# One gather tile in 64 moved from GpSimd to SyncE, row by row, in the last layer of a graph network

## The reference, cut to what matters

```python
s = s @ W_up_s * inv; v = einsum('nui,uw->nwi', v, W_up_v) * inv   # per node
h = silu(silu(edge_feats @ A1 + b1) @ A2 + b2)                     # per edge
w0, w1, w2, w3 = split(h @ A3, 4, axis=1)
ss, vs = s[sender], v[sender]                                      # the gather
mji = concat(ss*y_s*w0, (vs . y_v)/R3*w3, ss*y_v*w1, vs*y_s*w2)
message = segment_sum(mji, receiver) / 10
```

## Time and profile before

| what | value |
|---|---|
| runs | 7211.72 us median of 3 (7203.6 to 7215.84) |
| profiled execution, span from first to last instruction | 7212.5 us |
| gathers of the message layer, first start to last start | 6068.1 to 7146.5 us |
| the last block's first matmul | 7159.95 us |
| POOL busy in the whole span | 4972.2 us (69%) |
| DMA in the message layer | 22% of 16 DMA engines, 56 GB/s |

### The profile page before, as it was taken

One profiled execution on the slowest core, in us unless ns is written; L12 is line 12 of the kernel. 1 busy time (PEld: TensorE's weight loads), 2 busy tenths in 40 slices (PEclk: granted clock), 3 DMA queues, 4 the chain that ended last, 5 costly groups with the idle time before them and its releaser, 6 DMA issues. The chain is left out here.

```text
span 7212.5 us, 119527 instructions
## 1 busy us (share of the span) xinstructions
PE 5515.6 (76%) x30306; PEld 4153.5 (58%) x30345; DVE 4706.7 (65%) x20339; ACT 2265.8 (31%) x5973; POOL 4972.2 (69%) x5179
## 2 busy tenths in 40 slices
PE   5675667776777766777777776789899997889887
PEld 4442344555666555566656665666666665667665
DVE  7985668466666446666636666664544546888887
ACT  1044442211114311113421111543333333554454
POOL 5777765677777477777577777647576574777774
PEclk6687888788888878888878888889999998988898
DMA  9433352577777467767557777657566773222222
GB/s 306 135 79 88 78 114 52 155 204 207 206 208 218 149 186 210 208 203 216 175 165 210 208 208 206 204 164 211 166 208 188 210 208 93 56 57 56 56 57 54
DMA packets 911842, 1151.30 MB, mean 160 GB/s; under 512 B 143281, under 2 KB 676465, under 8 KB 911249
## 3 DMA queue, kind: packets, MB, share of 16 engines
q1 hardware_dynamic: 689440, 673.54, 30.9%
q0 software_dynamic: 202464, 461.07, 23.9%
q10 hardware_dynamic: 19346, 9.66, 0.5%
HBM read 882.09 MB, written 261.74 MB: 159 GB/s over the span
## 5 line engine op out<-in xcount | busy, mean ns | idle before, releaser
L500 POOL DMA_INDIRECT G<-table_kv,idx x2496 | 2383.7, 955 | 966.5 <-issue 753.8
L1710 DVE SCALAR_TENSOR_TENSOR sums<-ramp,place,bank 128x128 f32<-128x128 f32 x2496 | 717.4, 342 | 1192.0 <-PE bank L1629 1098.4
L1619 PE MATMUL bank<-ident,G 128*128 128x128 f32 x2496 | 637.9, 334 | 720.1 <-DMA G<-table_kv,idx 713.5
L2144 POOL DMA_INDIRECT G<-table_h,src_idx x864 | 828.4, 959 | 465.0 <-issue 252.0
L1598 ACT COPY slab<-bank 128x512 f32<-128x512 f32 x624 | 364.8, 585 | 2295.3 <-PE bank L1619 2294.6
L500 POOL DMA_INDIRECT G<-table_h,idx x832 | 826.3, 993 | 298.2 <-issue 226.7
L1629 PE MATMUL bank<-qT,slab 128*128 x4992 | 915.5, 341 | 100.3 <-issue 80.4
L1629 PEld LDWEIGHTS bank<-qT,slab 128*128 128x128 f32 x4992 | 803.1, 244 | 196.0 <-issue 195.2
L1619 PEld LDWEIGHTS bank<-ident,G 128*128 128x128 f32 x2496 | 377.6, 163 | 931.2 <-DMA G<-table_kv,idx 891.7
L1841 DVE TENSOR_SCALAR OH<-ramp,place,weight 128x128 f32<-128x128 f32 x2076 | 715.4, 354 | 15.6 <-issue 8.5
L2128 PE MATMUL bank<-sums,qT 128*128 128x418 bf16 (+1 forms) x3528 | 676.4, 334 | 38.7 <-DVE same L2051 13.9
(11 more groups left out here) (355 smaller groups left out, 9538.6 us busy)
## 6 DMA issues: line engine op xcount, KB each, us to landing
stash<-G SPq DMA_DIRECT2D x312, 512.0 KB
sums<-stash SPq DMA_DIRECT2D x624, 256.0 KB
sums<-adjacency SPq DMA_DIRECT2D x294, 522.5 KB
adjacency<-same SPq DMA_DIRECT2D x49, 1184.0 KB, 13.9
same<-adjacency SPq DMA_DIRECT2D x90, 522.5 KB
G<-table_kv,idx POOLq DMA_INDIRECT x2496
sums<-adjacency SPq DMA_DIRECT2D x48, 408.0 KB
table_kv<-G SPq DMA_DIRECT2D x72, 256.0 KB, 3.2
```

What stands on the lines that cost most here:

```text
L500: pool.indirect_dma_start(G[:, s, 0:width], None, tab, bass.IndirectOffsetOnAxis(ap=idx[:, s:s + 1], axis=0)).then_inc(c_gather[s].sem, 16)
L1619: ins = pe.transpose(bank[q % 2][:, (s % QUAD) * P:(s % QUAD + 1) * P], G[:, s, 0:D], ident[:])
L1710: ins = dve.scalar_tensor_tensor(scratch[:, s, :], ramp[:], place[:, n * QUAD + s:n * QUAD + s + 1], bank[2 + q % 2][:, s * P:(s + 1) * P] ...
L2144: pool.indirect_dma_start(G[:, s, 0:D], None, table[l], bass.IndirectOffsetOnAxis(ap=src_idx[:, DENSE + t:DENSE + t + 1], axis=0)).then_in ...
```

## The change

GpSimd no longer gathers slot 15 in the last turn of every four (`FAR_TURNS = 4`): 13 tiles of 832, the far tiles. SyncE fetches them. The host adds the source numbers laid out by tiles in rows (`src_rows`). For each far tile SP loads one such row into `far_src`, and in each of the four turns, at four places, loads eight source numbers into registers and issues eight DMAs, each of one row of 512 bytes from `table[0]` into one partition of `far_rows` (two buffers). At the end of the fourth turn it waits until all 128 rows have landed and copies `far_rows` into slot 15 of `G` with one DMA. DVE waits for that copy (`far_landed`) in place of the gather. POOL's loop is written out over four turns.

```diff
             @block.gpsimd
             def _(_e):
-                gather_loop(table[0], D)
+                with pool.Fori(0, FAR_TILES) as m:
+                    for u in range(FAR_TURNS):
+                        for q in range(QUADS):
+                            pool.wait_ge(c_idx.sem, c_idx.turn(m, FAR_TURNS * QUADS, u * QUADS + q + 1))
+                            pool.sem_inc(c_issue.sem, 1)
+                            for s in range(q * QUAD, (q + 1) * QUAD):
+                                if u < FAR_TURNS - 1 or s != FAR_SLOT:
+                                    pool.indirect_dma_start(G[:, s, 0:D], None, table[0],
+                                                            bass.IndirectOffsetOnAxis(ap=idx[:, s:s + 1], axis=0)).then_inc(c_gather[s].sem, 16)
...
+                def far_line(m):
+                    t = (m * FAR_TURNS + FAR_TURNS - 1) * SLOTS + FAR_SLOT
+                    sp.dma_start(far_src[0:1, m % 2, :], a["src_rows"][t:t + 1, :]).then_inc(far_src_in.sem, 16)
+
+                def far_part(i, part):
+
+                    m, k = i // FAR_TURNS, (i % FAR_TURNS * QUAD + part) * FAR_ROWS
+                    if k == 0:
+                        sp.wait_ge(far_src_in.sem, far_src_in.at(16 * (m + 1)))
+                        if m + 1 < FAR_TILES:
+                            far_line(m + 1)
+                        if m >= 2:
+                            sp.wait_ge(far_landed.sem, far_landed.at(16 * (m - 1)))
+                    _, nodes = nc.values_load_multi_w_load_instructions(
+                        far_src[0:1, m % 2, k:k + FAR_ROWS], engines=(SP,), min_val=0, max_val=NODES - 1,
+                        skip_runtime_bounds_check_because="sources are nodes")
+                    for r, node in enumerate(nodes):
+                        sp.dma_start(far_rows[k + r:k + r + 1, m % 2, :], table[0][bass.ds(node, 1), :]).then_inc(far_in[m % 2].sem, 16)
+
+                def far_tile(i):
+                    m = i // FAR_TURNS
+                    sp.wait_ge(far_in[m % 2].sem, far_in[m % 2].at(16 * P * (m // 2 + 1)))
+                    sp.wait_ge(c_msg.sem, c_msg.at(QUADS * i))
+                    sp.dma_start(G[:, FAR_SLOT, 0:D], far_rows[:, m % 2, :]).then_inc(far_landed.sem, 16)
+
+                far_line(0)
 
                 def turn(i, last):
                     for h in range(2):
                         sp.wait_ge(c_msg.sem, c_msg.turn(i, QUADS, 2 * h + 2 - QUADS))
                         sp.dma_start(ea[:, h, :, :].rearrange("p s c -> p (s c)"),
                                      a["edge_attrs"][:, bass.ds(i * SLOTS * 4 + h * HALF * 4, HALF * 4)]).then_inc(c_ea[h].sem, 16)
+                        far_part(i, 2 * h)
                         if not last:
                             sp.wait_ge(c_h1.sem, c_h1.turn(i, 2, h + 1))
                             features(h, (i * 2 + (h + 2)) * PAIR)
+                        far_part(i, 2 * h + 1)
+                    if i % FAR_TURNS == FAR_TURNS - 1:
+                        far_tile(i)
                 turns(turn)
...
                 def messages(i, turn_q):
                     j, h, q = turn_q % 2, turn_q % QUADS // 2, turn_q % QUADS
                     dve.wait_ge(c_rows.sem, c_rows.turn(i, QUADS, turn_q + 1 - QUADS))
+                    t = i + turn_q // QUADS
+                    far = (t + 1) // FAR_TURNS
                     for s in range(q * QUAD, (q + 1) * QUAD):
-                        dve.wait_ge(c_gather[s].sem, c_gather[s].turn(i, 16, 16 * (1 + turn_q // QUADS)))
+                        if s != FAR_SLOT:
+                            dve.wait_ge(c_gather[s].sem, c_gather[s].at(16 * (t + 1)))
+                        elif t % FAR_TURNS == FAR_TURNS - 1:
+                            dve.wait_ge(far_landed.sem, far_landed.at(16 * far))
+                        else:
+                            dve.wait_ge(c_gather[s].sem, c_gather[s].at(16 * (t + 1 - far)))
```

More of the change, by code:

```diff
@@ L98 @@
 KNOTS = BLOCKS + 1
+FAR_TURNS = 4
+FAR_TILES = TURNS // FAR_TURNS
+FAR_SLOT = SLOTS - 1
+FAR_ROWS = P // (FAR_TURNS * QUAD)
 assert CHUNK * CHUNKS == NP and CHUNK <= 512 and TILES % 8 == 0
@@ L104 @@
 assert 8 * ZERO_COLS >= ADJ_COLS and 8 * ZERO_COLS <= ADJ_PITCH and FIRST_BLOCKS * DENSE <= GROUP_COLS <= MASK_COLS and EXTRA_BLOCKS * HALF_DENSE <= MASK_COLS and TURNS_DENSE % 2 == 0 and P < SEEN
-assert sum(PIECE_LENGTHS) == TURNS and PT <= P and 3 * PIECES * P <= BLOCKS * ROW
+assert sum(PIECE_LENGTHS) == TURNS and FAR_TILES * FAR_TURNS == TURNS and FAR_ROWS * FAR_TURNS * QUAD == P and PT <= P and 3 * PIECES * P <= BLOCKS * ROW
 assert PART * X_PARTS == BLOCKS and NODES % BN == 0 and NODES // BN <= BLOCKS
@@ L203, in build_program @@
         per_slot = sb("per_slot", [P, 2, SLOTS])
+        far_rows = sb("far_rows", [P, 2, D])
+        far_src = sb("far_src", [P, 2, P], I32)
         stats = sb("stats", [P, BLOCKS, 6])
@@ L326, in build_program @@
         c_tp = signal("tp_psum")
+        far_src_in = signal("far_src_in")
+        far_landed = signal("far_tile_landed")
+        far_in = [signal(f"far_rows_in{k}") for k in range(2)]
         c_far = signal("distance")
@@ L2784 @@
         "src_tile": np.concatenate([tiles(src), np.zeros((P, SLOTS), src.dtype)], axis=1),
+        "src_rows": src.reshape(TILES, P),
         "dst_tile": tiles(dst),
```

## The result

| | kernel before | changed kernel |
|---|---|---|
| median, lowest, highest of 13 runs each | 7208.59 (7201.88 to 7215.84) us | 7190.18 (7180.83 to 7198.58) us |
| ratio, 95% interval | | 0.9975 (0.9968 to 0.9983) |
| profiled execution, span | 7212.5 us | 7179.0 us |

The change made the kernel 18 us faster, 0.25%, where 157 us slower was predicted. It went the way of the first rival: SP stayed hidden, and POOL's 13 gathers were the gain. The two profiled executions lie 33.5 us apart, but 20.1 us of that were gone before the message layer began: its first gather starts at 6048.0 us where it was 6068.1 us, and nothing ahead of it was changed.

A forecast was written before the change was run, and what follows sets the result against it. POOL's gathers bound the message layer, 83.0 us a group of four turns; SP's added work, 95.2 us against POOL's 81.7, would become the bound, adding 156.7 us to 7212.5 us: 7369 us, range 7195 to 7500 us.

The forecast's parts named there:

- the first rival: Message layer: SP stays hidden and POOL's gain of 16.9 us is real, giving 7196 us; chance 0.10.
- item 1 of what the change adds on SP: SP's 128 one-row DMAs a group: 0.19 us ahead plus 0.43 us issue, 0.62 us a row, 79.4 us.
- DMAs that back up: Rival on SP's queue: packs of eight rows issue at 0.60 us each, giving 7651 us; chance 0.14 from 0.50 us up.
- S: SP's in-order work for a group of four turns in the message layer, summed to 95.2 us.
- The eight numbers of a register load: SP's 16 loads of eight source numbers a group: 0.36 us each, 0.40 with gap, 6.4 us together.
- The register work ahead of a row: On SP before each row's DMA: gap, MOVE and ALU_OP for a new node number, 0.19 us.
- The landing at a group's end: SP stands still until the group's last row has landed: 2.0 us less the issue itself, 1.6 us.
- POOL's 1.297 us a gather: POOL's gather spacing in the message layer; 13 gathers fewer save 16.9 us if POOL remains the bound.
- the formula 13 x S - 1080.9: Change of the kernel's time in us from SP's group sum over 13 groups; nothing at a sum of 83.1 us.
- The signs that the prediction had named for being wrong: Changed profile: rows 0.51 us apart or closer, SP still waiting for DVE, DVE waiting 0.5 us a quad, POOL gaps 0.30 us.
- where the wait shows: DVE waits several us at quad 3 of every fourth turn for SP's copy; late `ea` copies cost nothing of their own.
- One engine, a dearer row?: SP's rows, if each goes through one DMA engine like L941, issue at 0.49 us, giving 7468 us.

The follow-up runs named there:

- run 5: Kernel before plus a series of small SP DMAs and register loads ahead of its output; one-partition issue 0.24 us alone, 128 partitions 0.35 us.
- run 1: Kernel before with only POOL's loop written out over four turns, all 832 gathers kept: 7209.31 us, ratio 1.0001.
- run 2: Changed kernel with the 13 gathers dropped and SP fetching nothing: 7188.10 us, ratio 0.9973 to the kernel before.
- run 9: Changed kernel with one of every eight rows fetched twice, 16 rows more in a group: 7190.84 us, ratio 0.9974 to the kernel before.
- run 10: Changed kernel with four of every eight rows fetched twice, 64 rows more in a group: 7371.74 us, ratio 1.0235 to the kernel before.
- run 11: Changed kernel with ACT also fetching six tiles row by row, POOL gathering 813: 7174.76 us, ratio 0.9958 to the kernel before.

## Why the prediction was wrong

**The step that failed** is in item 1 of what the change adds on SP, *the issue*: "no DMA of a single row into one partition is in the trace ... I take 0.43 us". It is 0.228 us, below the lower end of 0.31 us. Every row from which the price was taken, but L941's, was of a DMA to 8 partitions or more, most to 16, 64 or 128, and run 5 shows that those cost 0.27 to 0.60 us where one of one partition costs 0.23 to 0.25 us, back to back or not. The one row of a single partition, L941, was read as a sign that such a transfer is dearer, and it isn't. Even the 0.60 us of `biasc`, put down to DMAs that back up, was mostly that of 64 partitions: 0.47 us alone, and only 0.13 us more back to back. The term is 128 x (0.43 - 0.228) = 25.9 us of S too much.

**The eight numbers of a register load** were mis-sized the other way: 0.717 us and not 0.36, so with its gap 0.77 us, 12.3 us in a group where 6.4 stood. The rows of one and four numbers had given 0.012 us for each more; from four to sixteen it is 0.055 us. The floor of about 600 ns that the Trainium skill gives a register load ("DMA: Bandwidth & Descriptors", section "Latency and other measured facts") would have come nearer for this load, but it isn't a floor: SP's loads of one number take 0.273 us. With 0.77 us a load the issue at which the gain is gone is 0.290 us and not 0.336 us; 0.228 us is well under both. With both terms as measured S is 95.2 - 25.9 + 5.9 = 75.2 us, under POOL's 81.7 us, and the prediction's own order of waits gives the hidden case.

**What held.** The register work ahead of a row was 0.19 us and measured 0.412 - 0.228 = 0.184 us. The landing at a group's end was put at 1.6 us and measured 1.0 us (13.0 us in 13 waits). POOL's 1.297 us a gather as the value of each one dropped: runs 1 and 2. The loop at nothing: run 1. SP's order as one sum, a break-even somewhere between 80 and 96 us, and the formula 13 x S - 1080.9: runs 9 and 10, of which the one with an SP group a little under 81.7 us moves nothing and the one at 95.8 us gives +167 us, where the prediction had +157 us for 95.2 us. The time that the first rival gave, 7196 us, stands against 7190.2 us; as a difference, 16.9 us against 18.4 us by the medians and 12 to 23 us by the interval. It had a chance of 0.10. The measured 7190.2 us lies 5 us under the range's lower end, 7195 us, which did take in the gain on POOL; 3.9 of these are the base, 7212.5 us in the sum and 7208.6 us as the median of 13 runs. The signs that the prediction had named for being wrong are all there: rows 0.41 us apart, SP waiting for DVE in 75 halves of turns, DVE waiting 0.47 us a quad for gathers, POOL's gaps 0.30 us.

**What held in part** is where the wait shows. The prediction had DVE stand at quad 3 of every fourth turn, and late copies of `ea` cost nothing. In run 10 DVE stands there (103.6 us in 13 waits, one for each far tile) but more in all for `ea`, 167.8 us in 65 waits. SP's order is one chain and the sum is the same, but the place isn't.

**One engine, a dearer row?** The Trainium skill says that a transfer of a single row and element gets one engine ("DMA: Bandwidth & Descriptors", section "Why a DMA increments its semaphore by 16 and not by 1"), and the prediction made a dearer row of it (7468 us). The runs show the opposite of that reading: the fewest partitions, the cheapest issue. Whether what counts are partitions, descriptors or engines, no run here tells.

## What to carry to other kernels

Work moved to an idle queue has to be added up as one in-order sum and set against the time that the bound gives it; that sum decided here, and where SP was the bound it gave +164.5 us for +166.7 us (155 to 184 us by the interval). Its price per piece is worth nothing if it is taken from pieces of another shape: a DMA to one partition is issued in 0.23 us and one to 16 or more in 0.31 to 0.60 us, so look first for a row of the same shape, and where there is none, measure it before trusting a margin of some tenths of a microsecond times 1664. An engine whose issue rate sets the pace can be relieved in small pieces by queues that have room, as by SP and ACT here (run 11), until these sums meet the pace.

## What the runs showed of the hardware that was not expected

- A DMA into 64 partitions took 0.47 us to issue alone and 0.60 us back to back, more than one into 128 (0.35 and 0.43 us).
- Two numbers took longer to load into registers (0.65 us) than four (0.48 us), by a single row each.
- Not every chip runs the kernel before alike: 7205 to 7210 us here in three series, 9587 us on another chip, with waits that nothing in the profile releases. There SP needed 115.4 us for a group of 144 rows that was worked out at 80.0 us, and the versions with more instructions on SP or ACT were 1.5 to 2.4% slower than the kernel before.
